# Attention in 64-row product pairs, with the mask moved from TensorE to VectorE's maximum and ScalarE's bias

## What is computed

```python
dots = jnp.einsum('bhid,bhjd->bhij', q, k) * SCALE
m = jax.nn.softmax(dots, axis=-1)
diag = jnp.diagonal(m, axis1=-2, axis2=-1)
mu = diag.mean(axis=-1, keepdims=True)
sd = diag.std(axis=-1, ddof=1, keepdims=True)
keep = jnp.abs((diag - mu) / sd) <= Z_THRESH
valid = keep[..., :, None] & keep[..., None, :]
masked = jnp.where(valid, dots, NEG)
attn = jax.nn.softmax(masked, axis=-1)
row_any = jnp.any(valid, axis=-1, keepdims=True)
attn = jnp.where(row_any, attn, 0.0)
out = jnp.einsum('bhij,bhjd->bhid', attn, v)
```

## Time and profile before

| what | value |
|---|---|
| median of 3 runs | 1997.17 us (1995.05 to 1997.43) |
| profiled execution, its own time | 1995.78 us |
| its span | 1994.5 us |
| PE busy | 1876.0 us, 94% |
| DVE, ACT, POOL busy | 1383.4, 1146.8, 1192.7 us |
| attention's exponentials (L2035), first to last | 793.2 to 1855.2 us |

### The profile page before, as it was taken

One profiled execution on the slowest core, in us unless ns is written; L12 is line 12 of the kernel. 1 busy time (PEld: TensorE's weight loads), 2 busy tenths in 40 slices (PEclk: granted clock), 3 DMA queues, 4 the chain that ended last, 5 costly groups with the idle time before them and its releaser, 6 DMA issues. The chain is left out here.

```text
span 1994.5 us, 22434 instructions
## 1 busy us (share of the span) xinstructions
PE 1876.0 (94%) x7526; PEld 1304.8 (65%) x7526; DVE 1383.4 (69%) x2237; ACT 1146.8 (57%) x1715; POOL 1192.7 (60%) x676
## 2 busy tenths in 40 slices
PE   8998999889998987999999999999999999998888
PEld 5873444336876745777777777777777777765466
DVE  5618899976427745677776777777777777775576
ACT  5327787645335455666666666666666666653544
POOL 5542867863535452575666666666667666667454
PEclk9999999999999998999999999999999999999999
DMA  2000000000010033313131322222231313100100
GB/s 95 1 0 0 0 0 0 1 0 0 1 47 1 1 85 72 67 45 73 45 72 45 73 45 55 62 56 62 43 74 40 77 40 71 44 6 12 53 6 17
DMA packets 45684, 74.29 MB, mean 37 GB/s; under 512 B 26560, under 2 KB 28224, under 8 KB 45312
## 3 DMA queue, kind: packets, MB, share of 16 engines
q1 hardware_dynamic: 45104, 72.26, 15.6%
q10 hardware_dynamic: 432, 0.59, 0.1%
q0 software_dynamic: 32, 0.00, 0.0%
HBM read 20.66 MB, written 1.18 MB: 11 GB/s over the span
## 5 line engine op out<-in xcount | busy, mean ns | idle before, releaser
L2270 POOL TENSOR_TENSOR at_e_lo<-at_e,at_e_hi 128x1024 fp32r<-128x1024 f32 x256 | 614.3, 2400 | 377.8 <-DVE at_e_hi L2235 374.4
L2035 ACT ACTIVATE at_e<-at_ps 128x1024 f32<-128x1024 f32 x256 | 262.6, 1026 | 267.1 <-PE at_ps L1937 267.1
L2027 ACT ACTIVATE at_ps<-at_ps,at_neg_diag 128x1024 f32<-128x1024 f32 x256 | 278.6, 1088 | 78.7 <-DVE at_neg_diag L2124 74.8
L2131 DVE TENSOR_REDUCE at_row_max<-at_ps 128x1 f32<-128x1024 f32 x256 | 311.4, 1216 | 5.4 <-PE at_ps L1918 5.3
L2235 DVE CAST at_e_hi<-at_e 128x1024 fp32r<-128x1024 f32 x256 | 257.6, 1006 | 37.2 <-ACT at_e L2035 37.1
L2124 DVE CUSTOM_DVE_ANT_0 at_junk_diag<-at_ps,ident 128x128 bf16<-128x128 f32 x256 | 74.2, 290 | 250.0 <-PE at_ps L1890 249.8
L1056 POOL TENSOR_TENSOR mb_work<-mb_work,mb_c 128x1024 f32<-128x1024 f32 x64 | 151.7, 2370 | 96.5 <-DVE mb_work L1025 94.3
L421 POOL TENSOR_TENSOR ffn_lo<-ffn_hid,ffn_hi 128x512 fp32r<-128x512 f32 x96 | 127.3, 1330 | 130.9 <-DVE ffn_hi L338 130.9
L1950 PE MATMUL at_pv_ps<-at_e_hi,at_v_hi 128*128 128x512 f32 x512 | 176.0, 425 | 0.3 <-ACT at_pv_sb L2074 0.3
L1918 PE MATMUL at_ps<-at_k,at_q 128*128 128x512 f32 x512 | 163.5, 401 | 10.6 <-DVE at_row_max L2131 7.4
L1888 PE MATMUL at_ps<-at_k,at_q 128*128 128x512 f32 x512 | 162.6, 399 | 9.6 <-ACT at_ps L2027 4.0
(11 more groups left out here) (369 smaller groups left out, 3858.5 us busy)
## 6 DMA issues: line engine op xcount, KB each, us to landing
at_q<-at_qk_hi SPq DMA_DIRECT2D x64, 256.0 KB, 3.6
at_k<-at_qk_hi SPq DMA_DIRECT2D x32, 512.0 KB, 5.9
at_q<-at_qk_lo SPq DMA_DIRECT2D x32, 256.0 KB, 6.5
at_k<-at_qk_lo SPq DMA_DIRECT2D x32, 256.0 KB, 6.3
at_recips<-at_recip_row SPq DMA_DIRECT2D x31, 256.0 KB, 3.4
ffn_h_raw<-in_h SPq DMA_DIRECT2D x2, 1024.0 KB, 7.2
at_head_w_raw<-in_w_qkv SPq DMA_DIRECT2D x32, 64.0 KB, 4.2
x<-in_x SPq DMA_DIRECT2D x4, 256.0 KB, 6.6
```

Source lines behind the costliest of these rows:

```text
L2027: act.eng.activation(ps[:], ps[:], ACT.Exp, scale=SCALE, bias=m.small["neg_diag"][s][:, blk:blk + 1], accum_out=m.small["sums"][s][:, blk: ...
L2035: act.eng.activation(m.e[e % 2][:], slot("turned_scores", h, blk)[:], ACT.Exp, scale=SCALE).then_inc(sem["at_exp"])
L2131: dve.eng.tensor_reduce(m.small["row_max"][h % SLOTS][:, blk:blk + 1], slot("best", h, blk)[:], AX.X, ALU.max).then_inc(sem["at_best_out"])
L2270: pool.eng.tensor_tensor(m.e_lo[e % 3][:], m.e[e % 2][:], m.e_hi[e % 3][:].bitcast(F32), ALU.subtract).then_inc(sem["at_lo"])
```

## The change

Products of 64-row operands (scores, best, turned_scores) no longer fill 128 rows with a second pair of operands. The tiles m.qk hold q in rows 0 to 63 and k in 64 to 127, m.kq the same swapped. A product on rows 0 to 63 writes one bank and one on rows 64 to 127 the other. Scores are three such pairs, best one, turned_scores three and one pair for the shift. Sums over 128 rows (weigh, project, values, project_out) are made as 64-row pairs too, in two passes: straight (top rows to bank 0, low rows to bank 1), then turned (top to bank 1, low to bank 0). The turned pass waits on a semaphore that the straight pass's last product raises. Between the two passes of weigh stand best and the straight pass of project, values or project_out. Steps without both weigh and best keep the old form (the _alone functions).

The mask leaves the products: it goes through DRAM to all 128 partitions as bf16 (spread_mask), DVE adds it inside the maximum with one tensor_tensor_reduce, and ACT adds it for the keys as the bias of exps. mean, square, turn_mask and turn_shift become two small products each, stand ahead of scores, and share a ring slot with best. AT_TURNED goes from 23 to 22. move_parts has 4 transfers.

```diff
-AT_TURNED, AT_PV, AT_PV_OUT, AT_RECIP, AT_SPREAD, AT_NORM, AT_OUT = 23, 24, 32, 34, 35, 37, 39
+AT_TURNED, AT_PV, AT_PV_OUT, AT_RECIP, AT_SPREAD, AT_NORM, AT_OUT = 22, 24, 32, 34, 35, 37, 39
...
+        if small or best:
+            order.append([(*small, 0)] if small else [])
+            if best:
+                order[-1].append(("best", *best))
...
+    n = m.slot_no[kind, h, k]
+    if kind == "best" and len(m.slot_order[n]) == 2:
+        small, sh, _ = m.slot_order[n][0]
+        small_read(pe, c, small, sh)
...
+    def spread_mask(h):
+        sp.wait_ge(sem["mask_move"], 16 * (h + 1))
+        sp.wait_ge(sem["at_best_out"], (h - 1) * BLK)
+        sp.wait_ge(sem["mask_spread"], 16 * h)
+        sp.eng.dma_start(m.mask[h % 2][:], m.mask_dram[h % 2].broadcast_to([P, SEQ])).then_inc(sem["mask_spread"], 16)
...
+        sp.wait_ge(sem["at_spare"], 5)
+        for n, rows in enumerate(ROWS):
+            row = m.shift[h % 2][rows.start:rows.start + 1, :].bitcast(F32).rearrange("a (b q) -> a b q", b=BLK // 2)
+            sp.eng.dma_start(row, m.shift_rows[h % 2][n * (BLK // 2):(n + 1) * (BLK // 2), :].bitcast(F32)
+                             ).then_inc(sem[f"shift_move{h % 2}"], 16)
...
+    def ends_straight(mm, user):
+        mm.then_inc(sem["at_straight"])
+        straight[user] = max(straight) + 1
...
+    def after_straight(user):
+        pe.wait_ge(sem["at_straight"], straight[user])
...
+    def both_rows(banks, w, x, first, last, turned=False):
+        order = banks[::-1] if turned else banks
+        for rows, bank, moving in zip(ROWS, order, x[::-1] if turned else x):
+            mm = pe.eng.matmul(bank, w[rows], moving[rows], start=first, stop=last)
+        return mm
...
-        for hf in range(2):
-            pe.eng.matmul(ps[:, HALF[hf]], q[:, CROSS, rows], k[:, CROSS, HALF[hf]], start=True, stop=False)
-        for hf in range(2):
-            mm = pe.eng.matmul(ps[:, HALF[hf]], q[:, MAIN, rows], k[:, MAIN, HALF[hf]], start=False, stop=True)
+        for n, (q, k) in enumerate(((HI, HI), (LO, HI), (HI, LO))):
+            pe.eng.matmul(ps[:, HALF[0]], own[TOP, q, rows], swapped[TOP, k, HALF[0]], start=(n == 0), stop=(n == 2))
+            mm = pe.eng.matmul(ps[:, HALF[1]], swapped[LOW, q, rows], own[LOW, k, HALF[1]], start=(n == 0), stop=(n == 2))
         mm.then_inc(sem["at_scores"])
...
+        pe.eng.matmul(ps[:, HALF[0]], own[TOP, HI, rows], swapped[TOP, HI, HALF[0]], start=True, stop=True)
+        pe.eng.matmul(ps[:, HALF[1]], swapped[LOW, HI, rows], own[LOW, HI, HALF[1]], start=True,
+                      stop=True).then_inc(sem["at_best"])
...
+        for n, (k, q) in enumerate(((HI, HI), (LO, HI), (HI, LO))):
+            pe.eng.matmul(ps[:, HALF[0]], swapped[TOP, k, keys], own[TOP, q, HALF[0]], start=(n == 0), stop=False)
+            pe.eng.matmul(ps[:, HALF[1]], own[LOW, k, keys], swapped[LOW, q, HALF[1]], start=(n == 0), stop=False)
+        pe.wait_ge(sem["at_spare"], 5)
+        pe.wait_ge(sem[f"shift_move{h % 2}"], 2 * 16 * (h // 2 + 1))
+        both_rows([ps[:, half] for half in HALF], m.minus, [m.shift[h % 2]] * 2, False,
+                  True).then_inc(sem["at_turned_scores"])
...
+        if turned:
+            after_straight(WEIGH)
+        elif e:
+            pe.wait_ge(sem["at_pv"], e)
+        banks = [m.pv_ps[:, half] for half in HALF]
+        both_rows(banks, with_ones, [hi[:, half] for half in HALF], blk == 0 and not turned, False, turned)
+        both_rows([bank[0:HD] for bank in banks], m.v_lo[:, blk, i, :], [hi[:, half] for half in HALF], False, False, turned)
+        pe.wait_ge(sem["at_lo"], e + 1)
+        mm = both_rows(banks, with_ones, [lo[:, half] for half in HALF], False, blk == BLK - 1 and turned, turned)
+        if turned:
+            mm.then_inc(sem["at_pv"])
+        else:
+            ends_straight(mm, WEIGH)
...
+        weighed, tested = due(t, AT_PV, BLK), due(t, AT_BEST, BLK)
+        apart = bool(weighed and tested)
         if at := due(t, AT_TURNED, BLK):
             turned_scores(*at)
...
+        if at := due(t, AT_SCORES, BLK):
+            scores(*at)
+        if apart:
+            weigh(*weighed, False)
+        if tested:
+            best(*tested)
+        for turned in (False, True):
+            if at := due(t, AT_QK):
+                if apart:
...
+            if apart and not turned:
+                weigh(*weighed, True)
+        if weighed and not apart:
+            weigh_alone(*weighed)
...
+        act.eng.activation(m.e[e % 2][:], slot("turned_scores", h, blk)[:], ACT.Exp, scale=SCALE,
+                           bias=m.small["dropped"][h % SLOTS][:, blk:blk + 1]).then_inc(sem["at_exp"])
...
+        ps = slot("best", h, blk)
         dve.wait_ge(sem["at_best"], h * BLK + blk + 1)
-        dve.eng.tensor_reduce(m.small["row_max"][h % SLOTS][:, blk:blk + 1], slot("best", h, blk)[:], AX.X,
-                              ALU.max).then_inc(sem["at_best_out"])
+        dve.wait_ge(sem["mask_spread"], 16 * (h + 1))
+        dve.eng.tensor_tensor_reduce(
+            out=ps[:], in0=ps[:], in1=m.mask[h % 2][:], scale=1.0, scalar=-BIG, op0=ALU.add, op1=ALU.max,
+            accum_out=m.small["row_max"][h % SLOTS][:, blk:blk + 1]).then_inc(sem["at_best_out"])
...
                 dve.eng.tensor_tensor(c.x[:, cols], c.x[:, cols], slot("out", h)[:], ALU.add).then_inc(sem["x_attn"])
+        if at := due(t, AT_MEAN):
+            negate_mean(at[0])
+        if at := due(t, AT_SQUARE):
+            negate_square(at[0])
+        if at := due(t, AT_MASK):
+            mask_rows(at[0])
+        if at := due(t, AT_SHIFT):
+            shift_rows(at[0])
```

More of the change, by code:

```diff
@@ L1591, in pair_due, with small_due @@
     return at[0] if at and at[0] % 2 == 1 else None
+def small_due(t):
+    for kind, offset in (("mean", AT_MEAN), ("square", AT_SQUARE), ("turn_mask", AT_MASK), ("turn_shift", AT_SHIFT)):
+        if at := due(t, offset):
+            return kind, at[0]
+    return None
 def attention_slots():
-    order = []
+    order, number = [], {}
     for t in range(AT_FIRST, AT_LAST):
+        small, best = small_due(t), due(t, AT_BEST, BLK)
         if at := due(t, AT_TURNED, BLK):
-            order.append(("turned_scores", *at))
+            order.append([("turned_scores", *at)])
@@ L1621, in slot_free, with small_read @@
-def slot_free(pe, c, m, kind, h, k=0):
-    n = m.slot_no[kind, h, k] - 3
-    if n < 0:
+            order.append([("out", h, 0)])
+    for n, keys in enumerate(order):
+        for key in keys:
+            number[key] = n
+    return order, number
+def small_read(pe, c, kind, h):
+    stats = {"mean": 3, "square": 4}
+    if kind == "turn_mask":
+        pe.wait_ge(c.sem["at_mask"], h + 1)
+    elif kind == "turn_shift":
+        pe.wait_ge(c.sem["at_shift"], h + 1)
+    else:
+        pe.wait_ge(c.sem["at_stats"], STATS * h + stats[kind])
@@ L1958, in weigh, with project_out, project_out_alone @@
         mm.then_inc(sem["at_pv"])
-    def project_out(h):
+    def project_out(h, turned):
+        pair = h % HEADS // 2
+        ps = slot("out", h)
+        if turned:
+            after_straight(OTHER)
+        else:
+            pe.wait_ge(sem["attn_out_load"], 16)
+            pe.wait_ge(sem["at_norm"], h + 1)
+            slot_free(pe, c, m, "out", h)
+        mm = both_rows([ps[:, half] for half in HALF], m.w_out[:, pair, :], [m.heads_out[:, half] for half in HALF],
+                       not turned, turned, turned)
+        if turned:
+            mm.then_inc(sem["at_out"])
+        else:
+            ends_straight(mm, OTHER)
+    def project_out_alone(h):
         pair = h % HEADS // 2
@@ L2323, in attention @@
         m.recips = sb("at_recips", [HD, SEQ])
-        m.qk_hi = sb("at_qk_hi", [P, SEQ], F32R)
-        m.qk_lo = sb("at_qk_lo", [P, SEQ], F32R)
+        m.mask = [sb(f"at_mask{i}", [P, SEQ], BF16) for i in range(2)]
         m.e_hi = [sb(f"at_e_hi{i}", [P, SEQ], F32R) for i in range(3)]
```

305 lines of the change are left out of this document (160 added, 145 removed).

## The result

The changed kernel takes **1982.06 us** (median of 4 runs, 1980.71 to 1983.15) against 1996.47 for the one before, measured beside it: a ratio of **0.9932**, 95% interval 0.9921 to 0.9944. It is faster by 0.7%; the forecast was 2016 us and rather slower. The profiled execution took 1980.71 us, with a span of 1979.4.

The account below looks back on a forecast made before the run. PE was taken as the bound. Per head -3.66 + 1.0 + 0.4 + 0.25 + 2.8 = +0.8 us, +23 over 29 heads, -4 outside: 2016 us. Own range 1957 to 2104; with rivals 1940 to 2104, far ends left out.

Parts of the forecast that it names:

- A pair costs one slot: Two 64-row products on different row halves together take one 512-column product's PE time, 0.229 us; saves 3.66 us a head.
- Mean waits: In step 1 of a head, PE stalls at mean until qk_lo is done: 1.6 us (1.4 to 1.7).
- Turn_mask waits: In step 3 of a head, PE stalls at turn_mask for keeps, which follows best on DVE: 1.2 us (0.8 to 1.6).
- heads_out's 0.4: Steps 5 to 7: POOL's heads_out delays a DVE cast, best comes late and PE waits for its ring slot, 0.4 us.
- What PE gets in addition: The prediction's step on added PE time per head: +1.0, +0.4 and +0.25 us.
- The turn: Weigh's second half waits for the last product of its first: 0.10 to 0.22 us a step, +1.0 a head.
- Four small products more: Four additional small products on PE per head, at 0.11 us each: +0.4 us a head (0.2 to 0.6).
- Values: Twice as many weight loads in values, which might queue: +0.25 us a head, between nothing and +0.72.
- square's wait for the deviations: In step 2 of a head, square stalls PE for ACT's deviations, late behind the sums: 0.3 us (0.1 to 0.5).
- Pairs faster than a slot: Rival: 64-row pairs on PE hide the weight change and run below 0.222 us; 1968 us, chance 0.22.
- Bad overlap: Rival: the two 64-row halves on PE overlap badly; 2660 us, or 2250 with a third lost; chance 0.08 together.
- DVE and POOL as the bound: Rival: DVE's cast loses its turn to POOL's product in most steps, +1.6 us a head; 2062 us, chance 0.10.

Follow-up runs that it names:

- the four orders tried here: Four reorderings of weigh's two passes in the 1903 us version, to cover the 0.11 us gap behind best: 1938.6, 1949.3, 1906.8 and 1904.6 us.

## Why the prediction was wrong

The forecast was 2016 us, slower than before; the measured time is 1982 us, faster. The head of 33.17 us lies between the 34.3 that was to show the forecast right and the 33 below which it was to be wrong.

**Right.** A pair costs one slot: 0.229, with both halves running. The plain step lost two slots for 0.11 of gap. Mean waits 1.56 us for qk_lo (said: 1.6), as here in the changed kernel's timeline:

```profile
1237.71 0.41 PE L1878 MATMUL at_ps<-at_shift_row,at_minus 64*128 64x512 f32 x2
...
1238.32 1.23 DVE L2237 TENSOR_TENSOR at_qk<-at_ps,at_qk 128x1024 fp32r<-128x1024 f32 x1 [1.64 <-ACT at_qk L2142]
...
1239.69 0.27 PE L1965 MATMUL at_ps<-at_row_sum_parts,at_ones 64*128 64x2 f32 x2 [1.56 <-DVE at_qk L2237]
...
1239.79 0.47 PE L1957 MATMUL at_ps<-at_kq,at_qk 64*128 64x512 f32 x1
...
1248.04 0.22 PE L1972 MATMUL at_ps<-ident,at_dropped 64*8 64x64 f32 x2 [1.10 <-DVE at_dropped L2295]
```

Turn_mask waits 1.1 (24.2 / 22; said: 1.2), but in 8 of the heads it waits for v_lo instead, up to 1.5, which was not foreseen. The waits for maxima at scores and best, where heads_out's 0.4 was to show, are (4.5 + 4.4) / 31 = 0.3. DVE's addition, move_parts' transfers and the mask's way through DRAM are hidden, as said: from 788 to 1813 us PE waits for no transfer but the shift's (0.8 us), and DVE for none.

**The step that failed is "What PE gets in addition"**, three terms that were all sized too high:
- *The turn*, +1.0: it is 0.11 x 6.5 = 0.7. The bounds were 0.10 for halves that start together and 0.22 for staggered ones; the prediction took the middle, and the halves start together.
- *Four small products more*, +0.4: nothing that these rows show. The two of a pair go side by side, and mean's pair holds scores up by 0.10 (1239.69 to 1239.79), as one product did by 0.11.
- *Values*, +0.25: nothing. The timeline of PE in the changed kernel:

```profile
1209.54 0.28 PE L1927 MATMUL at_ps<-at_wv_hi,at_xn_hi 64*128 64x256 f32 x2
1209.66 0.27 PE L1927 MATMUL at_ps<-at_wv_hi,at_xn_lo 64*128 64x256 f32 x2
1209.77 0.28 PE L1927 MATMUL at_ps<-at_wv_lo,at_xn_hi 64*128 64x256 f32 x2
```

Six such pairs of 256 columns follow each other at 0.12, like the single products of the earlier trace rows, each with two weight loads.

That is 0.7 in place of 1.65: 0.95 x 29 heads = 28 us. The waits are 3.05 - 0.67 = +2.4 in place of +2.8 (square's wait for the deviations, 0.3, did not come). But each wait costs more than the view counts, since idle time begins there at the modelled end of the product before: mean could have followed at 1237.71 + 0.23 = 1237.94 and started at 1239.69, 1.75 later, for 1.56 in the view. In four such places, one of them in the kernel before, it is 0.15 to 0.19 more; 54 waits more at 0.17 make, as an estimate, some 0.3 a head that the prediction did not have. The two together are 0.1 a head, 3 us, less. Outside the heads it was -5.8 instead of -4. From 2016 these take 28, 3 and 2: 1983, against 1982 measured. A head then changes by -3.66 + 0.7 + 2.4 + 0.3 = -0.3, as found. The sign hung on a remainder of 0.8 between -3.66 and +4.45.

Two readings of the kernel before were off without moving the forecast. The 17th record in the window of the earlier trace rows is the end of the product before it, not a small product; the slot stays 0.229. And project_out was put at 0.46 a head: with what it holds up behind it, it takes about 1.7 us every second head, 0.86 a head, before (1233.77 to 1235.94, less 0.46 for two products of weigh) as after (1229.42 to 1230.51 and 1230.97 to 1232.07, less 0.23 each), so it drops out of the difference.

**The rivals.** Pairs faster than a slot: no, 0.229; the kernel became faster for another reason. Bad overlap: no, by the same 0.229. By the Trainium skill ("TensorE: Matmul & The Clock Gate", section "Measured speedup vs the span model") the estimate was 240 us more; its figure is for four 32-row tiles, and the trace shows no such loss for two halves of 64 rows. DVE and POOL as the bound: no; PE's waits for maxima come to 10.6 us from 788 to 1813 us, and none of its waits there is for e_lo.

What is not shown: why the first product behind a wait or a small product is followed only 0.31 to 0.34 later (in the kernel before as well), and how much of the 2.2 us ahead of the first turn_shift belongs to the mask's longer way.

## What to carry to other kernels

When a kernel bound by one engine is changed, the reordering can cost as much as the work removed: here 3.66 us a head were saved and 2.4 lost to waits, nearly all to three at once, for results that had become late against their reader, and moving the readers and their sources gave 4% more (1903 us) without touching the arithmetic. When a forecast is a small remainder of large terms, take each added cost where the nearest row puts it, and let the chance of either sign say how little the remainder is worth. In the four orders tried here, closing a small gap on the bound engine gave nothing, as each time something else moved nearer to its due time.
